# Group statistics from raw sums with their roots on GpSimd, ScalarE left to normalise, and both weight folds ahead of the spectra

## The chip, the cores and the metric

The kernel runs on one core of a Trainium2 chip. Its time is the device time of one execution in microseconds. The engines are TensorE (PE; PEld is its weight load), VectorE (DVE), ScalarE (ACT), GpSimd (POOL) and SyncE (SP), which here only issues transfers.

## What is computed

The input is (16, 16, 16, 256) float32: batch, time, width, channels. Three stages follow one another, and each adds to its input: a spectral mixing of the group-normalised input, causal attention over the 256 positions of each batch, and a mixture of eight experts of which each token takes two. The change lies wholly in the first stage and in the two weight products of the second.

```
def _gn(v, G=32, eps=1e-05):                       # groups of 8 channels, statistics over time and width
    g = v.reshape(B_, H_, W_, G, C_ // G)
    m = jnp.mean(g, axis=(1, 2, 4), keepdims=True)
    s = jnp.var(g, axis=(1, 2, 4), keepdims=True)
    return ((g - m) / jnp.sqrt(s + eps)).reshape(v.shape)
# spectral stage on xn = _gn(x)
x_ft = jnp.fft.rfft(xn, axis=-1)[..., :16]
out = x_ft * w_temb[None]                          # w_temb: time weights, sin/cos embedding @ ke_weights + ke_bias
out = jnp.einsum('btix,iox->btox', out, w)         # w: mixing weights, complex
norm = jnp.einsum('tix,iox->tox', jnp.abs(w_temb), jnp.abs(w)) + 1e-12
out = out / (jax.nn.relu(norm - 1.0) + 1.0)[None]
x = x + jnp.fft.irfft(pad(out), n=256, axis=-1)
# attention on _ln_t(x): scores from x Wq^T Wk x^T, output through Wv and Wo
# experts: softmax router, top 2 of 8, gelu, float32
```

## The kernel before

Each engine runs its own hand-written program; semaphores alone order them, and each engine executes strictly in the order written. There is no scheduler. The text below names semaphores as the code does.

**The opening (first stage).** The input lies channel-major in `xc`, 128 channels by 2 halves by 4096 tokens, and arrives in four chunks of four batches each (`ld_xc[c]`). A chunk has 8 tiles of 128x256 (`gn_tile`): four batches by two channel halves. For every chunk DVE takes the statistics of its 8 tiles (`gn_statistics`, bn_stats into `gst`), merges them into mean and variance per channel (`gn_moments`, bn_aggr into `gmv`), and turns the variance into a second moment. PE then multiplies them by a 128x128 matrix that averages 8 neighbouring channels (`group_means`, into the bank `psO`). DVE forms the group variance (`gn_variance`), ACT takes its root (L600), DVE the reciprocal and the shift (`gn_scale`), and ACT normalises the tiles in place (L604); of the last chunk DVE normalises four tiles itself (L892).

Beside that, DVE computes the angles of the time embedding (L807 to L815, then `emb_ready`), ACT its sine (L593), PE and DVE the time weights (`time_weights`), and POOL spreads the mixing weights into block matrices (L474, four each for `mix_r` and `mix_i`, L479 for `mix_abs`). The sizes of the mixing weights go DVE (L819, L821), ACT (a root, L595), DVE (`wabs_sum`, L874), POOL (L479), PE (L1259, the norm), DVE (`inv`, L884).

When the first two chunks are normalised PE takes the spectra of the first half of the positions (`spectra(0)`, L1247), and when all are, those of the second (`spectra(1)`). DVE multiplies them by the time weights (L902), PE mixes them (L1279, 32 matmuls of 256 columns), and DVE divides by the norm (L911), after which `spec` is complete and the first inverse transform can run (L1295).

**Attention.** 16 batches pass in a software pipeline of slots (`run_attention`). Ahead of it PE forms the two weight products, `fold(wq, wk)` and `fold(wv, wo_t)` (L1237, four matmuls each), one behind the mixing, one behind the first inverse transform; ACT copies them out (L612).

**Experts.** 39 groups of 256 rows, with the weights of five experts loaded while attention runs (SP, L431).

In float32 one matmul instruction shows as two records of PE and two of PEld; counts like "x8" for four matmuls are such records.

## Time and profile before

| | |
|---|---|
| median of 3 runs | 723.77 us (722.03 to 724.03) |
| the profiled execution, its own time | 726.27 us |
| its span, first to last instruction | 724.5 us |
| busy: PE, PEld | 647.4, 624.2 us |
| busy: DVE, ACT, POOL | 516.5, 413.7, 429.6 us |
| mean granted clock of TensorE | 0.964 of full speed |

The span and the execution's own time differ by 1.8 us, which lie around the first and the last instruction. The span splits into the opening (to about 57 us), attention (to about 205 us), a transition in which slots are planned (to about 242 us) and the experts. Busy shares over the whole span are averages over these four and say little about the opening, so the rows that count are those of the timeline of each engine.

### The profile page before, as it was taken

The page shows a single profiled execution, that of the slowest core. Times are in us where ns is not written, and L with a number is a line of the kernel's source. Part 1 is how long each engine was busy: PE and PEld are TensorE (multiplying, and loading weights), DVE is VectorE, ACT ScalarE, POOL GpSimd, SP SyncE. Part 2 cuts the span into 40 slices and gives each one's busy share as a digit, 9 for nine tenths or more (in the row PEclk, how much of TensorE's full clock was granted, in tenths as well). Part 3 has the DMA queues.
Part 4 walks back from the last instruction along what each step waited for, and adds up shares of the span by engine and source line. Part 5 has one row for each costly group of instructions (what it writes and reads, how often), then busy time and mean ns, then how long its engine had stood idle before and what let it go on. Part 6 is the DMA issues. An engine that isn't in the chain of part 4 may idle for free. (4 is left out here: it accounts for less than half of the span.)

```text
span 724.5 us, 16522 instructions
## 1 busy us (share of the span) xinstructions
PE 647.4 (89%) x5010; PEld 624.2 (86%) x5010; DVE 516.5 (71%) x1217; ACT 413.7 (57%) x703; POOL 429.6 (59%) x340
## 2 busy tenths in 40 slices
PE   0496999999940699999999999999999999999993
PEld 0385888888840599999999999999999999999993
DVE  8764577777764577787878777877787777777761
ACT  1804777766520556566666656565656565756550
POOL 5002326777666256766666666767676767676763
PEclk9999999999975799999999999999999999999998
DMA  8805752222323454433131313222222222232312
GB/s 343 273 0 186 276 179 74 92 90 97 106 105 113 136 162 146 96 108 59 29 59 31 57 31 57 41 47 45 43 49 39 51 37 52 36 53 35 57 19 29
DMA packets 39486, 64.13 MB, mean 89 GB/s; under 512 B 3808, under 2 KB 34848, under 8 KB 38304
## 3 DMA queue, kind: packets, MB, share of 16 engines
q0 software_dynamic: 14304, 18.92, 14.7%
q1 hardware_dynamic: 14816, 34.55, 13.5%
q10 hardware_dynamic: 10336, 10.31, 5.6%
q8 instruction: 13, 0.21, 0.1%
q14 instruction: 17, 0.14, 0.1%
HBM read 37.96 MB, written 25.81 MB: 88 GB/s over the span
## 5 line engine op out<-in xcount | busy, mean ns | idle before, releaser
L574 POOL TENSOR_TENSOR pj_lo<-w_ffn,pj_hi 128x1024 fp32r<-128x1024 f32 x78 | 189.1, 2425 | 122.8 <-ACT pj_hi L615 106.3
L1167 DVE TENSOR_TENSOR fc_lo<-w_ffn,fc_hi 128x1024 fp32r<-128x1024 f32 x78 | 116.1, 1527 | 86.2 <-ACT fc_hi L615 86.2
L564 POOL DMA_INDIRECT out<-y,add_id x78 | 121.9, 1563 | 45.1 <-issue 43.7
L615 ACT ACTIVATE pj_hi<-w_ffn 128x1024 fp32r x78 | 82.7, 1060 | 94.9 <-PE psO L1464 89.3
L615 ACT ACTIVATE fc_hi<-w_ffn 128x1024 fp32r x78 | 78.3, 1051 | 43.4 <-issue 43.4
L1464 PE MATMUL psP<-pj_hi,h_hi 128*128 128x256 f32 x312 | 91.5, 293 | 0.2 <-DVE h_lo L1167 0.2
L1464 PE MATMUL psP<-pj_hi,h_lo 128*128 128x256 f32 x312 | 88.5, 284 | 0.0
L1464 PE MATMUL psO<-pj_hi,h_lo 128*128 128x256 f32 x312 | 88.3, 283 | 0.0
L1464 PE MATMUL psO<-pj_lo,h_hi 128*128 128x256 f32 x312 | 88.3, 283 | 0.0
L1464 PE MATMUL psP<-pj_lo,h_hi 128*128 128x256 f32 x312 | 88.3, 283 | 0.0
L1464 PE MATMUL psO<-pj_hi,h_hi 128*128 128x256 f32 x312 | 88.1, 282 | 0.0
L528 POOL DMA_INDIRECT slots<-rows,slot x64 | 63.5, 993 | 19.1 <-issue 15.5
L1447 PE MATMUL psT<-x_hi,fc_hi 128*128 128x256 f32 x312 | 63.8, 287 | 5.0 <-DVE x_lo L1167 5.0
L1447 PE MATMUL psT<-x_lo,fc_hi 128*128 128x256 f32 x312 | 63.5, 286 | 0.0
L1447 PE MATMUL psT<-x_hi,fc_lo 128*128 128x256 f32 x312 | 63.5, 286 | 0.0
L1464 PEld LDWEIGHTS psP<-pj_hi,h_hi 128*128 128x128 f32 x312 | 59.8, 192 | 0.4 <-issue 0.4
L1464 PEld LDWEIGHTS psO<-pj_hi,h_hi 128*128 128x128 f32 x312 | 59.9, 192 | 0.0
L1464 PEld LDWEIGHTS psP<-pj_lo,h_hi 128*128 128x128 f32 x312 | 59.9, 192 | 0.0
L1464 PEld LDWEIGHTS psP<-pj_hi,h_lo 128*128 128x128 f32 x312 | 59.7, 191 | 0.0
L1464 PEld LDWEIGHTS psO<-pj_hi,h_lo 128*128 128x128 f32 x312 | 59.7, 191 | 0.0
L1464 PEld LDWEIGHTS psO<-pj_lo,h_hi 128*128 128x128 f32 x312 | 59.7, 191 | 0.0
L740 ACT ACTIVATE psT<-psT 128x512 f32<-128x512 f32 x78 | 45.3, 581 | 23.6 <-PE psT L1447 23.6
(252 smaller groups left out, 1639.4 us busy)
## 6 DMA issues: line engine op xcount, KB each, us to landing
w_ffn<-in_w_ffn SPq DMA_DIRECT2D x8, 2048.0 KB, 8.2
xg<-slots ACTq DMA_DIRECT2D x38, 265.0 KB
xc<-in_x_ch SPq DMA_DIRECT2D x4, 1024.0 KB, 8.9
out<-x SPq DMA_DIRECT2D x16, 256.0 KB
x<-in_x_tok SPq DMA_DIRECT2D x1, 3072.0 KB, 25.2
slots<-fill SPq DMA_DIRECT2D x9, 265.0 KB, 2.8
out<-y,add_id POOLq DMA_INDIRECT x78, 3.9
w_in<-in_w_in SPq DMA_DIRECT2D x1, 1024.0 KB, 13.7
```

The lines of the kernel that those rows point to most:

```text
L528: nc.gpsimd.indirect_dma_start(slots_d, bass.IndirectOffsetOnAxis(ap=slot[:, j, n, t % PT:t % PT + 1], axis=0), rows[:, t, :], None).then_ ...
L564: nc.gpsimd.indirect_dma_start(out_d, bass.IndirectOffsetOnAxis(ap=add_id[:, s:s + 1], axis=0), y[:, s, :], None, compute_op=ALU.add).then ...
L574: nc.gpsimd.tensor_tensor(pj_lo[:, 4 * a:4 * a + 4, :], w_ffn[:, bass.ds(e, 1), (2 + a) * DFF:(3 + a) * DFF].rearrange("p a (c d) -> p (a ...
L615: nc.scalar.activation(out, src, ACT.Copy, **kw).then_inc(done, 1)
L740: nc.scalar.activation(banks[c][:, :], banks[c][:, :], ACT.Gelu).then_inc(gelu_done, 1)
L1167: v.tensor_tensor(out, whole, upper.bitcast(F32), ALU.subtract).then_inc(done, 1)
L1447: ins = mm(banks[c][:, (f % 2) * GS:(f % 2 + 1) * GS], w[:, hh, f * P:(f + 1) * P], m[:, hh, :], start=(n == 0), stop=(n == 5))
L1464: ins = mm(bank[:, 0:D], w[:, f, s * P:(s + 1) * P], m[:, f, :], start=(f == 0 and n == 0), stop=(f == FC - 1 and n == 2))
```

## The change

The statistics are no longer merged on DVE. bn_stats leaves, for each half of a tile, a count, a mean and a sum of squared deviations. The changed kernel squares the two means into the places of the counts (`gn_squares`, one instruction), and `group_means` multiplies the raw numbers by two matrices in four matmuls that accumulate in one bank (`psS` and `psP` in turn). `gn_variance` is three instructions. The reciprocal root is one power on POOL (`inverse_root`), placed between the spreadings of the mixing weights. ACT has no root of the variance left. DVE normalises six tiles of the last chunk. Both folds stand ahead of the spectra, in banks `psO` and `psI`; the mixing into these banks waits until ACT has copied them. POOL begins to spread only after `emb_ready`. The squares of the mixing weights come behind the statistics of the second chunk, and their sum behind those of the third. SP's weight loads also wait for `idft_ready`. `conv_in` grows by the second averaging matrix, 128 columns.

```diff
-CONV_PARTS = (NG * WI * 2, NG * WI * 2, 3 * MC, DH * MC, P, 2)
+CONV_PARTS = (NG * WI * 2, NG * WI * 2, 3 * MC, DH * MC, 2 * P, 2)
+        def gn_bank(c):
+            return (psS, psP)[c % 2]
+        GN_BY_DVE = 6
...
+            pool.wait_ge(emb_ready, 1)
             pool.wait_ge(ld_conv, 16)
...
+            def inverse_root(c):
+                pool.wait_ge(gn_var, c + 1)
+                nc.gpsimd.tensor_tensor(grs[:, c, :], gvar[:, c, :], power[:, :], ALU.pow).then_inc(gn_inv, 1)
+            for g in range(NG):
+                mixing(mixr_w, mix_r, 0, g)
+            inverse_root(0)
+            for g in range(2):
+                mixing(mixi_w, mix_i, 1, g)
+            inverse_root(1)
+            for g in range(2, NG):
+                mixing(mixi_w, mix_i, 1, g)
+            inverse_root(2)
             pool.wait_ge(wabs_summed, 1)
...
+            inverse_root(3)
...
-            act.wait_ge(wabs_step, 2)
-            nc.scalar.activation(wabs[:, :], wsq[:, :], ACT.Sqrt).then_inc(wabs_ready, 1)
             act.wait_ge(temb_step, 4)
             nc.scalar.activation(tabs[:, :], tpow[:, :], ACT.Sqrt).then_inc(temb_ready, 1)
+
             for c in range(CHUNKS):
-                act.wait_ge(gn_var, c + 1)
-                nc.scalar.activation(gsd[:, c, :], gvar[:, c, :], ACT.Sqrt).then_inc(gn_sd, 1)
+                if c == 2:
+                    act.wait_ge(wabs_step, 2)
+                    nc.scalar.activation(wabs[:, :], wsq[:, :], ACT.Sqrt).then_inc(wabs_ready, 1)
                 act.wait_ge(gn_rs, c + 1)
...
+            def gn_squares(c):
+                dve.wait_ge(gn_raw, c + 1)
+                means, counts = gst[:, c, :, 1:6:3], gst[:, c, :, 0:6:3]
+                v.tensor_tensor(counts, means, means, ALU.mult).then_inc(gn_stats, 1)
             def gn_variance(c):
+
                 dve.wait_ge(gn_mm, c + 1)
...
+                v.tensor_copy(gmu[:, c, :], bank[:, CT:2 * CT]).then_inc(gn_sq, 1)
...
+                v.tensor_tensor(gsq[:, c, :], bank[:, CT:2 * CT], gmu[:, c, :], ALU.mult).then_inc(gn_sq, 1)
...
+                v.scalar_tensor_tensor(gvar[:, c, :], bank[:, 0:CT], GN_EPS, gsq[:, c, :], ALU.add,
+                                       ALU.subtract).then_inc(gn_var, 1)
+            def gn_shift(c):
+                dve.wait_ge(gn_inv, c + 1)
+                v.scalar_tensor_tensor(gnb[:, c, :], gmu[:, c, :], -1.0, grs[:, c, :], ALU.mult, ALU.mult).then_inc(gn_rs, 1)
+            gn_statistics(0, range(CT))
+            gn_squares(0)
             time_weights()
+            gn_variance(0)
             for c in range(1, CHUNKS):
+                gn_statistics(c, range(4))
+                if c > 1:
+                    gn_variance(c - 1)
+                else:
+                    gn_shift(0)
+                gn_statistics(c, range(4, CT))
+                gn_squares(c)
+                if c > 1:
+                    gn_shift(c - 1)
+                if c == 1:
+                    wabs_squares()
+                if c == 2:
+                    wabs_total()
             gn_variance(CHUNKS - 1)
+            gn_shift(CHUNKS - 1)
...
+            group_means(0)
+            group_means(1)
+            pe.wait_ge(ld_qkvo, 16)
+            fold(wq, wk, psO)
+            group_means(2)
+            fold(wv, wo_t, psI)
 
             pe.wait_ge(temb_step, 2)
             pe.wait_ge(gn_done, 2 * CT)
-            spectra(0)
-            pe.wait_ge(gn_done, 3 * CT + CT // 2)
-            pe.wait_ge(gn_done_dve, CT // 2)
+            spectra(0, range(0, 2))
+            group_means(CHUNKS - 1)
+            spectra(0, range(2, NG))
+            norms()
+            pe.wait_ge(gn_done, 4 * CT - GN_BY_DVE)
+            pe.wait_ge(gn_done_dve, GN_BY_DVE)
             spectra(1)
```

What stands in a row on each engine is shown at three places. DVE before, from the moments of the second chunk to the statistics of the last (`gst` are the raw statistics, `ggm` the group means, `gnb` the shift whose end releases ACT):

```order
L868 SCALAR_TENSOR_TENSOR gnb<-ggm,grs 128x8
L845 BN_STATS gst<-xc 128x6 x8
L859 COPY ggm<-psO 128x16
L860 TENSOR_TENSOR gsq<-ggm 128x8
L861 TENSOR_TENSOR gvar<-ggm,gsq 128x8
L862 TENSOR_SCALAR gvar<-gvar 128x8
L851 BN_AGGR gmv<-gst 128x2 x8
L854 TENSOR_TENSOR gsq<-gmv 128x8
L855 TENSOR_TENSOR gmv<-gmv,gsq 128x8
L867 RECIPROCAL grs<-gsd 128x8
L868 SCALAR_TENSOR_TENSOR gnb<-ggm,grs 128x8
L845 BN_STATS gst<-xc 128x6 x8
```

DVE now, over the same stretch, from the variance of the second chunk (bank `psP`) to that of the third (`psS`):

```order
L883 COPY gmu<-psP 128x8
L885 TENSOR_TENSOR gsq<-psP,gmu 128x8
L887 SCALAR_TENSOR_TENSOR gvar<-psP,gsq 128x8
L869 BN_STATS gst<-xc 128x6 x4
L877 TENSOR_TENSOR gst<-gst 128x16
L893 SCALAR_TENSOR_TENSOR gnb<-gmu,grs 128x8
L851 TENSOR_REDUCE wabs_sum<-wabs 128x16
L869 BN_STATS gst<-xc 128x6 x4
L883 COPY gmu<-psS 128x8
L885 TENSOR_TENSOR gsq<-psS,gmu 128x8
```

The sum `wabs_sum`, which stood ahead of the second chunk's statistics, now stands between the second chunk's shift and the last chunk's statistics. ACT before, from the sine to the third chunk:

```order
L593 ACTIVATE emb<-ang 32x16
L595 ACT_TABLE_LOAD
L595 ACTIVATE wabs<-wsq 128x64
L597 ACTIVATE tabs<-tpow 128x16
L600 ACTIVATE gsd<-gvar 128x8
L604 ACTIVATE xc<-xc,gnb,grs 128x256 x8
L600 ACTIVATE gsd<-gvar 128x8
L604 ACTIVATE xc<-xc,gnb,grs 128x256 x8
```

and ACT now:

```order
L616 ACTIVATE emb<-ang 32x16
L618 ACT_TABLE_LOAD
L618 ACTIVATE tabs<-tpow 128x16
L627 ACTIVATE xc<-xc,gnb,grs 128x256 x16
L623 ACTIVATE wabs<-wsq 128x64
L627 ACTIVATE xc<-xc,gnb,grs 128x256 x10
```

The root `wabs`, which `wabs_sum` reads, moved from ahead of all tiles to behind the sixteenth. PE now, from the first averages to the second half of the spectra (before, the three `group_means` had no fold between them, and the folds stood behind the mixing):

```order
L1266 MATMUL psP<-gst,conv_in 128x16 x2
L1268 MATMUL psP<-gst,conv_in 128x8
L1269 MATMUL psP<-gst,conv_in 128x8
L1274 MATMUL psO<-w_in 128x256 x4
L1266 MATMUL psS<-gst,conv_in 128x16 x2
L1268 MATMUL psS<-gst,conv_in 128x8
L1269 MATMUL psS<-gst,conv_in 128x8
L1274 MATMUL psI<-w_in 128x256 x4
L1284 MATMUL psT<-xc,conv_in 32x128 x16
```

Each chunk's averages are four matmuls where there was one, and the two folds stand around those of the third chunk.

## Rows read from the trace of the kernel before

**Rows 1.** The page: busy time by engine, and PE over 40 slices of the span.

```profile
PE 647.4 (89%) x5010; PEld 624.2 (86%) x5010; DVE 516.5 (71%) x1217; ACT 413.7 (57%) x703; POOL 429.6 (59%) x340
...
PE   0496999999940699999999999999999999999993
```

**Rows 2.** Windows: length, busy PE, PEld, DVE, ACT, POOL, then granted clock, DMA share, GB/s.

```profile
8.00:9.00 1.00, 0.00 (x0) 0.00 (x0) 1.00 (x4) 0.11 (x1) 1.00 (x2) 1.00 1.04 422
...
35.00:38.00 3.00, 3.00 (x54) 2.55 (x58) 1.51 (x4) 1.44 (x2) 0.00 (x0) 0.50 0.03 8
...
62.00:65.00 3.00, 2.74 (x10) 2.09 (x9) 1.77 (x6) 0.60 (x1) 1.10 (x2) 0.50 0.99 426
100.00:115.00 15.00, 15.00 (x98) 13.47 (x97) 11.81 (x53) 10.66 (x26) 5.88 (x8) 1.00 0.25 87
```

**Rows 3.** Timeline of DVE, opening: start, length, what, idle before it.

```profile
4.33 0.95 DVE L814 TENSOR_SCALAR ang<-ang,time_in 32x16 f32<-32x16 f32 x1
5.32 0.98 DVE L815 SCALAR_TENSOR_TENSOR ang<-ang,time_in 32x16 f32<-32x16 f32 x1
...
7.47 2.71 DVE L845 BATCH_NORM_STATS2 gst<-xc 128x6 f32<-128x256 f32 x8
...
16.71 0.17 DVE L859 COPY ggm<-psO 128x16 f32<-128x16 f32 x1
...
18.58 0.17 DVE L868 SCALAR_TENSOR_TENSOR gnb<-ggm,grs 128x8 f32<-128x8 f32 x1
...
32.39 0.20 DVE L867 RECIPROCAL grs<-gsd 128x8 f32<-128x8 f32 x1 [2.36 <-ACT gsd L600]
...
32.85 1.38 DVE L892 TENSOR_SCALAR xc<-xc,ggm,grs 128x256 f32<-128x256 f32 x4
```

**Rows 4.** Timeline of ACT, opening.

```profile
7.85 0.26 ACT L595 ACTIVATE wabs<-wsq 128x64 f32<-128x64 f32 x1
...
18.78 4.04 ACT L604 ACTIVATE xc<-xc,gnb,grs 128x256 f32<-128x256 f32 x8 [1.05 <-DVE gnb L868]
...
32.84 2.07 ACT L604 ACTIVATE xc<-xc,gnb,grs 128x256 f32<-128x256 f32 x4 [0.49 <-DVE gnb L868]
```

**Rows 5.** Timeline of POOL: spreading, opening.

```profile
4.21 4.22 POOL L474 TENSOR_TENSOR mix_r<-conv_in 128x512 f32<-128x512 f32 x4 [3.33 <-DMA conv_in<-in_conv_in]
```

**Rows 6.** POOL's groups, shapes apart: the power of two columns, a copy.

```profile
L505 POOL TENSOR_TENSOR rs<-rs,power 128x2 f32<-128x2 f32 x32 | 22.7, 711 | 40.9 <-DVE rs L946 38.6 <-issue 2.3
L559 POOL COPY add_id<-slot_id 128x2 int32 x37 | 7.0, 189 | 0.0
```

**Rows 7.** Timeline of PE: opening and start of attention; last, one row of its middle.

```profile
23.64 1.87 PE L1259 MATMUL psI<-tabs,mix_abs 128*128 128x16 f32 x8
...
31.25 1.15 PE L1247 MATMUL psV<-xc,conv_in 128*32 128x128 f32 x16
34.97 2.11 PE L1247 MATMUL psT<-xc,conv_in 128*32 128x128 f32 x32 [2.58 <-ACT xc L604]
...
37.74 1.18 PE L1247 MATMUL psV<-xc,conv_in 128*32 128x128 f32 x16
38.85 0.70 PE L1279 MATMUL psS<-zr,mix_r 128*128 128x256 f32 x2
...
52.77 1.89 PE L1237 MATMUL psS<-w_in 128*128 128x256 f32 x8
...
61.65 0.78 PE L1307 MATMUL psT<-ident,xn 128*128 128x128 f32 x4 [2.83 <-ACT xn L674]
...
63.12 3.10 PE L1317 MATMUL psG<-xn_t,qk_w 128*128 128x256 f32 x8 [0.26 <-ACT xn_t L615]
...
103.43 0.96 PE L1336 MATMUL psT<-attn_in,xn_t 128*128 128x8 f32 x8
```

**Rows 8.** Transfers by line: KB each, us from issue to landing.

```profile
w_in<-in_w_in SPq DMA_DIRECT2D x1, 1024.0 KB, 13.7
```

**Rows 9.** Issue of the first chunk and its landing, window 1.6 to 2.1.

```profile
xc<-in_x_ch SPq DMA_DIRECT2D x1, 1024.0 KB, 5.8
...
1.69 0.43 SPq L411 DMA_DIRECT2D xc<-in_x_ch  x1
```

More of the change, by code:

```diff
@@ L108, in constants @@
     return {
-        "dft": dft.astype(f), "masks": masks.astype(f), "group": np.kron(np.eye(P // 8), np.full((8, 8), 1 / 8)).astype(f),
+        "dft": dft.astype(f), "masks": masks.astype(f), "group": np.concatenate([np.kron(np.eye(P // 8), np.full((8, 8), 1 / n)) for n in (16, 8 * SEQ)], axis=1).astype(f),
         "angles": angles.astype(f), "causal": causal.astype(f), "counting": counting.astype(f), "experts": experts.astype(f),
@@ L177, in hybrid_block @@
         dft = dft.rearrange("p (h m) -> p h m", h=DH)
+        group = group.rearrange("p (n q) -> p n q", n=2)
         idft = cv("idft", [MC, D])
@@ L209, in hybrid_block @@
         x = at("x", [P, NT, D])
[L210 removed]
+        power = at("power", [P, 8])
         attn_in = at("attn_in", [P, sum(ATTN_PARTS)])
@@ L848, in gn_moments @@
-            def gn_moments(c):
-                for n in range(CT):
-                    ins = v.bn_aggr(gmv[:, c, n, :], gst[:, c, n, :])
-                gn_link(ins)
-                mean, var = gmv[:, c, :, 0], gmv[:, c, :, 1]
-                gn_link(v.tensor_tensor(gsq[:, c, :], mean, mean, ALU.mult))
-                v.tensor_tensor(var, var, gsq[:, c, :], ALU.add).then_inc(gn_stats, 1)
+                if n == CT - 1:
+                    ins.then_inc(gn_raw, 1)
+            def gn_squares(c):
+                dve.wait_ge(gn_raw, c + 1)
+                means, counts = gst[:, c, :, 1:6:3], gst[:, c, :, 0:6:3]
+                v.tensor_tensor(counts, means, means, ALU.mult).then_inc(gn_stats, 1)
@@ L870, in _ @@
-            gn_statistics(0)
-            gn_moments(0)
-            dve.wait_ge(wabs_ready, 1)
-            v.tensor_reduce(wabs_sum[:, :], wabs[:, :].rearrange("p (g o) -> p o g", g=NG), AX_X, ALU.add).then_inc(wabs_summed, 1)
+                bank = gn_bank(c)
+                v.tensor_copy(gmu[:, c, :], bank[:, CT:2 * CT]).then_inc(gn_sq, 1)
+                dve.wait_ge(gn_sq, 2 * c + 1)
+                v.tensor_tensor(gsq[:, c, :], bank[:, CT:2 * CT], gmu[:, c, :], ALU.mult).then_inc(gn_sq, 1)
@@ new lines, in _ @@
+                if c == 1:
+                    wabs_squares()
+                if c == 2:
+                    wabs_total()
+            gn_variance(CHUNKS - 1)
+            gn_shift(CHUNKS - 1)
+            dve.wait_ge(gn_rs, CHUNKS)
+            for n in range(CT - GN_BY_DVE, CT):
+                tile = gn_tile(CHUNKS - 1, n)
+                v.tensor_scalar(tile, tile, grs[:, CHUNKS - 1, n:n + 1], gnb[:, CHUNKS - 1, n:n + 1], ALU.mult,
+                                ALU.add).then_inc(gn_done_dve, 1)
@@ L883, in _ @@
             dve.wait_ge(norm_mm, 1)
[L884 removed]
+            v.tensor_scalar(inv[:, :], psS[:, 2 * CT:2 * CT + NG * HT], 1e-12, 1.0, ALU.add, ALU.max).then_inc(inv_step, 1)
             dve.wait_ge(inv_step, 1)
             v.reciprocal(inv[:, :], inv[:, :]).then_inc(inv_ready, 1)
[L887 to L893 removed]
@@ L1228, in group_means @@
                 pe.wait_ge(gn_stats, c + 1)
-                if c:
-                    pe.wait_ge(gn_var, c)
-                mm(psO[:, 0:2 * CT], group[:, :], gmv[:, c, :, :], start=True, stop=True).then_inc(gn_mm, 1)
+                if c > 1:
+                    pe.wait_ge(gn_var, c - 1)
+                bank = gn_bank(c)
+                for n in range(2):
+                    mm(bank[:, 0:2 * CT], group[:, 0, :], gst[:, c, :, 3 * n:3 * n + 2].rearrange("p n k -> p k n"),
+                       start=(n == 0), stop=False)
+                mm(bank[:, 0:CT], group[:, 1, :], gst[:, c, :, 2], start=False, stop=False)
+                mm(bank[:, 0:CT], group[:, 1, :], gst[:, c, :, 5], start=False, stop=True).then_inc(gn_mm, 1)
             def fold(w, m, bank):
@@ L1239, in fold, with spectra @@
                 ins.then_inc(qkvo_mm, 1)
-            def spectra(half):
+            def spectra(half, groups=range(NG)):
                 cols = slice(half * SEQ // 2, (half + 1) * SEQ // 2)
-                for g in range(NG):
+                for g in groups:
                     for j in range(4):
```

102 lines of the change are left out of this document (37 added, 65 removed).

## The prediction

> **What bounds the kernel now.** I read the page first. PE is the busiest engine, and its slices are full from the fourth on, but for a dip in the middle [rows 1]; in the middle of attention a window of 15 us shows it busy all 15 us at the full granted clock [rows 2]. So attention and the experts run at PE's pace and are not touched by the change. What the opening gains or loses is passed on whole, as long as nothing at the start of attention swallows it. The chain of waits in the page covers only the last microseconds, so for the opening I read the timelines of the engines. There PE waits 2.58 us for the last normalised tiles and starts the second half of the spectra at 34.97 [rows 7]. **That start, 34.97, is the mark against which I reckon the change**, and the first mixing matmul at 38.85 the next one. Behind it nothing changes until attention but the places of the folds.
>
> What leads to 34.97: ACT needs 4.04 us for eight tiles, 0.505 each, and idles between chunks [rows 4]. DVE is the slower one. Its first statistics start at 7.47 and take 2.71; from the variance of the first chunk at 16.71 to the end of its shift at 18.75 it spends 2.04 us on small instructions, most of 0.17 [rows 3]. Per chunk that makes 4.7. At the end it waits 2.36 for ACT's root, then ACT takes four tiles in 2.07 and DVE four in 1.38 [rows 3, 4].
>
> **What the change removes.** Between two chunks' statistics DVE keeps one square (0.17), three for the variance (0.51) and one shift (0.17), with 0.04 between dependent ones about 1.05 us instead of 2.04. ACT's roots and the wait of 2.36 go. The embedding chain is also freed: L814 and L815 take 0.95 and 0.98 where their like take 0.17, and they end at 5.28 and 6.30, one spreading of 1.05 apart, that began on POOL at 4.21 [rows 3, 5]. A DVE instruction that reads SBUF beside POOL's product waits until that product is done; statistics do not (2.71 under the same cover). With POOL held back to `emb_ready`, this is ready near 4.75. But the first chunk lands at 1.69 + 5.8 = 7.49 [rows 9], 0.16 later with 64 KB more in front at 422 GB/s [rows 2], so the statistics start at 7.65 and nothing of this comes through.
>
> **What it adds, step by step, at a power of 0.72 us.** Chunk 0: statistics to 10.36, square to 10.57. The averages are four matmuls; the norm has just as many, and took 1.87 [rows 7]; done 12.5. Variance to 13.1, power to 13.9. The shift wants to run at 14.4, but POOL has started a spreading at 13.9 and holds it until 15.0. ACT starts its tiles there instead of at 18.78. Chunk 1: the rest of its statistics and square to 16.6, the two squares of the mixing weights, averages at 18.5, variance 19.1, power 19.9, statistics of chunk 2 to 20.4, square held to 21.0, shift held by the second spreading to **22.05**. ACT has been idle since 19.1.
>
> Now the order decides. ACT normalises chunk 1 until 26.1, then takes the root `wabs`, 0.26 [rows 4], and DVE, which stands at `wabs_sum` with the last statistics queued behind, **waits from 22.05 to 26.3**. Before, that sum stood ahead of all this and waited for nothing. Then: sum 26.6, half the statistics 27.9, variance 28.5, power 29.25, the other half 29.75; `mix_abs` on POOL (1.05) holds the square to 30.4, shift 30.6. ACT: chunk 2 and two tiles, 10 x 0.505, to **35.7**. DVE: averages (0.95 to 1.87), variance, power, shift 32.9 to 33.8, six tiles of 0.345, to **35.1 to 35.9**. PE: averages, 32 spectra records (2.0), norm (0.95 to 1.87): 34.3 to 36.2. So the spectra's second half starts at 35.7 to 36.2 instead of 34.97: **+0.7 to +1.2**. The earlier start of 3.7 us is spent in the wait of 4.3 and the three held shifts.
>
> **The power.** The trace has it only for two columns, 0.711 [rows 6]; here it has eight. Bound below: all of it is start-up, 0.71. Above: it grows in proportion beyond a copy of two columns (0.189), 0.189 + 4 x 0.522 = 2.3. POOL multiplies 512 columns in 1.05 [rows 5], so columns are cheap to it, and I take 1.0, nearer the lower. It counts about three times (chunks 0 and 1 through the held shifts, chunk 3 alone): the start goes to 36.5 to 37.2 at 1.0, and to 39.4 to 40.3 at 2.3. Taken: 36.6, **+1.6**.
>
> **The clock.** At 23.6 the profile's clock reads full, but eight records of weight-bound matmuls take 1.87 there and 0.96 in attention [rows 7]: the early stretch is at the lower level, 1.2 GHz. In 35 to 38 it is granted 0.50 [rows 2], after 2.58 idle. In the changed kernel the folds keep PE busy from 18.5 to 27 and the averages, spectra and norm from 30.4 on, so the second half will mostly run at 2.4 GHz. What is it worth? The last 16 records (from 37.74, 1.18) straddle the rise, the same ones of the first half (from 31.25, 1.15) were wholly at the lower level: no gain [rows 7]. I take 0 to -0.4, say **-0.2**. The Trainium skill ("TensorE: Matmul & The Clock Gate", The HAM clock gate) measures back-to-back matmuls twice as fast at the higher level; by that the half would take 1.94 instead of 3.88. The same section gives about 62 ns per matmul as the sequencer's floor where hardware decoding is off, which by 64 records in 3.88, 61 ns each, would leave it at 3.88.
>
> **The folds** (four matmuls, 1.89 each at full clock, about 3.5 at half) move into idle time of PE: the weights land at 4.0 + 13.7 = 17.7 [rows 8], and the last spectra wait for ACT at 26.1 anyway. Where they left they were covered as well: the first by DVE's division after 52.77, the second by the normalisation, behind which PE idled 2.83 before 61.65 [rows 7]. Worth 0. But they kept PE active: now it idles from the end of the mixing to 61.65 but for one inverse transform. It ran 62 to 65 at 0.50 already [rows 2], L1317 taking 3.10 against 1.89 of an equal fold; I add **+0.3**, between 0 and 1.7. ACT copies the folds at 36 to 37.5, before the mixing reaches psO. SP's loads start some 2 us earlier, behind nothing that PE waits for. POOL's inverse parts run at about 34 to 36, far before 55.
>
> **Sum.** +1.6 - 0.2 + 0.3 = +1.7 us. The profiled execution took 726.27, 2.5 over the median of 723.77; its own would become 728.0. On the median: 725.4.
>
> **The rivals.**
> - *The wait on the root costs what I say, and the power is cheap or middling* (0.7 to 1.3): +0.5 to +2.5, 724.3 to 726.3. Chance 0.47.
> - *The power grows with columns* (1.5 to 2.3): +2.5 to +5.3, up to 729. For it: 0.711 for two columns against 0.189 for a copy. Against it: 512 products in 1.05. Chance 0.23.
> - *Faster: the spectra are clock-bound after all.* PE has the folds in front, so the second half runs at 2.4 GHz and takes 1.94: -1.9 against +1.6 + 0.3, 723.8; with the power at 0.72 (+0.7) it is 722.8. It decides from the point where the start lies below 36.6. Past -2.2 it gets only if POOL's products do not hold the shifts either: without the holds the start is 33.6, -1.3, together -3.0, 720.8. For it: weight-bound rows halve. Against it: the group across the rise did not. Chance 0.18, of which 0.12 beyond the bound below.
> - *The start of attention stays one stretch longer at the lower clock*: +1.7 more, 727. Chance 0.12.
>
> A change under 0.3%, 2.2 us, can hardly be told from none. The first case lies mostly inside it; faster 0.13, same 0.47, slower 0.40. The range reaches from the fast rival's 721.5 to the slow power's 729.
>
> **What will show it.** Right: DVE idle 4 us ahead of `wabs_sum`, released by ACT; ACT idle some 4 us after its sixteenth tile; shifts of near 1 us ending with a POOL product; L1284's second half starting near 36.5. The power's mean at 128x8 settles the second case; the length of the second half (3.9 or 2) the third; L1365's first four matmuls (3.1 or more) the fourth. Wrong would be a sum that does not wait, or first mixing matmuls before 38.

## The result, and the profile after

The changed kernel is slower, by a little: ratio 1.0048 (95% 1.0036 to 1.0060) to the kernel before in the same session, or 3.5 us. Its median over nine runs is 726.62 us, against 722.05 for nine runs of the kernel before; two of its nine were disturbed by the machine (1670 and 756 us) and don't enter the ratio, and the median of the other seven is 725.89. Two later sessions gave 1.0031 and 1.0041. The profiled execution took 726.62, its span is 724.5; the forecast was 725.4.

The page's totals and the windows that answer to [rows 1, 2]; the last column but two is the granted clock:

```profile
PE 655.2 (90%) x5034; PEld 631.3 (87%) x5034; DVE 514.4 (71%) x1175; ACT 411.8 (57%) x697; POOL 435.7 (60%) x344
...
37.00:40.00 3.00, 2.86 (x52) 2.61 (x56) 2.35 (x8) 2.31 (x4) 0.00 (x0) 0.50 0.00 0
64.00:67.00 3.00, 2.74 (x9) 2.27 (x10) 1.27 (x3) 0.60 (x1) 1.10 (x2) 0.50 0.51 115
100.00:115.00 15.00, 15.00 (x95) 13.34 (x93) 12.03 (x61) 9.94 (x22) 4.47 (x7) 1.00 0.08 27
```

DVE and ACT each lost 2 us of work and POOL gained 6; attention's middle is unchanged. The totals say nothing of why it is slower. DVE's timeline of the opening does (answers to [rows 3]):

```profile
4.65 0.22 DVE L838 SCALAR_TENSOR_TENSOR ang<-ang,time_in 32x16 f32<-32x16 f32 x1
7.54 2.71 DVE L869 BATCH_NORM_STATS2 gst<-xc 128x6 f32<-128x256 f32 x8 [2.67 <-DMA xc<-in_x_ch]
12.49 0.17 DVE L883 COPY gmu<-psS 128x8 f32<-128x8 f32 x1 [1.32 <-PE psS L1269]
14.85 1.02 DVE L893 SCALAR_TENSOR_TENSOR gnb<-gmu,grs 128x8 f32<-128x8 f32 x1 [0.48 <-POOL grs L489]
...
21.29 0.18 DVE L877 TENSOR_TENSOR gst<-gst 128x16 f32<-128x16 f32 x1
21.70 1.00 DVE L893 SCALAR_TENSOR_TENSOR gnb<-gmu,grs 128x8 f32<-128x8 f32 x1 [0.22 <-POOL grs L489]
26.95 0.26 DVE L851 TENSOR_REDUCE wabs_sum<-wabs 128x16 f32<-128x64 f32 x1 [4.25 <-ACT wabs L623]
...
30.75 1.00 DVE L893 SCALAR_TENSOR_TENSOR gnb<-gmu,grs 128x8 f32<-128x8 f32 x1 [0.22 <-POOL grs L489]
...
34.37 2.63 DVE L919 TENSOR_SCALAR xc<-xc,grs,gnb 128x256 f32<-128x256 f32 x6
```

The embedding chain is freed, 0.22 each for L837 and L838 against 0.95 and 0.98 [rows 3], and nothing comes of it, since the first chunk still lands at 7.5. The row with 4.25 in its bracket is the wait at `wabs_sum`, released by ACT. The three shifts (L893) of 1.00 to 1.02 are the held ones. The fourth, of the last chunk, takes 0.33, from 34.01 on; no product runs then, but a cast of POOL's that ends at 34.31. A shift beside which POOL does nothing takes 0.17 (below). On ACT the other half of the same knot (answers to [rows 4]), and POOL with the powers and products that hold the shifts (answers to [rows 5, 6]):

```profile
15.91 4.04 ACT L627 ACTIVATE xc<-xc,gnb,grs 128x256 f32<-128x256 f32 x8 [4.48 <-DVE gnb L893]
22.74 4.04 ACT L627 ACTIVATE xc<-xc,gnb,grs 128x256 f32<-128x256 f32 x8 [2.79 <-DVE gnb L893]
26.68 0.24 ACT L623 ACTIVATE wabs<-wsq 128x64 f32<-128x64 f32 x1
31.79 5.04 ACT L627 ACTIVATE xc<-xc,gnb,grs 128x256 f32<-128x256 f32 x10 [4.87 <-DVE gnb L893]
```

```profile
13.14 1.68 POOL L489 TENSOR_TENSOR grs<-gvar,power 128x8 f32<-128x8 f32 x1 [4.10 <-DVE gvar L887]
14.80 2.06 POOL L481 TENSOR_TENSOR mix_i<-conv_in 128x512 f32<-128x512 f32 x2
20.02 1.64 POOL L489 TENSOR_TENSOR grs<-gvar,power 128x8 f32<-128x8 f32 x1 [3.17 <-DVE gvar L887]
21.63 2.07 POOL L481 TENSOR_TENSOR mix_i<-conv_in 128x512 f32<-128x512 f32 x2
```

PE (answers to [rows 7]) starts the spectra's second half, the mark of the prediction, at 37.14 instead of 34.97:

```profile
19.19 3.76 PE L1274 MATMUL psO<-w_in 128*128 128x256 f32 x8
...
23.86 1.97 PE L1274 MATMUL psI<-w_in 128*128 128x256 f32 x8
26.92 2.08 PE L1284 MATMUL psT<-xc,conv_in 128*32 128x128 f32 x32 [1.09 <-ACT xc L627]
...
33.56 1.07 PE L1296 MATMUL psS<-tabs,mix_abs 128*128 128x16 f32 x8
37.14 2.08 PE L1284 MATMUL psT<-xc,conv_in 128*32 128x128 f32 x32 [2.52 <-DVE xc L919]
...
41.03 0.70 PE L1327 MATMUL psS<-zr,mix_r 128*128 128x256 f32 x2
```

DVE's six tiles of the last chunk end last, at 37.00 (ACT's at 36.83), and the first two of them are held too, until POOL's cast and product for the inverse transform are done. These two tiles take 0.54 and 0.88, the other four 0.40 each:

```profile
34.37 0.54 DVE L919 TENSOR_SCALAR xc<-xc,grs,gnb 128x256 f32<-128x256 f32 x1
34.83 0.88 DVE L919 TENSOR_SCALAR xc<-xc,grs,gnb 128x256 f32<-128x256 f32 x1
34.84 0.72 POOL L515 TENSOR_TENSOR idft_parts<-idft,idft_parts 32x256 fp32r<-32x256 f32 x1
```

Where the loss goes from there is read from six marks of each profile. They are, in us: first statistics; the spectra's second half; attention's first value product (L1327 before, L1375 after); attention's last matmul row; the copy of `counts`; and, further on, the end of the last expert matmul.

| | stats | 2nd half | value | last | counts | end |
|---|---|---|---|---|---|---|
| before | 7.47 | 34.97 | 66.06 | 204.54 | 221.94 | 712.19 |
| before_again | 7.43 | 35.11 | 66.48 | 204.95 | 222.36 | 708.92 |
| before_third | 7.44 | 35.04 | 66.82 | 205.31 | 222.71 | 716.56 |
| after | 7.54 | 37.14 | 68.57 | 207.04 | 224.43 | 712.26 |
| again | 7.13 | 36.73 | 68.55 | 207.04 | 224.45 | 712.61 |
| after_third | 7.14 | 36.75 | 68.61 | 208.36 | 225.45 | 715.70 |

Against the first profile of before the end is where it was, though 2.5 us are lost by `counts`. That profile was a long one: its own time lies 2.5 us over the median, and the second one shows why (below). Against the second (own time 722.97), the change costs 2.03 at the mark, 2.09 at both ends of attention, 2.07 at `counts`, 3.34 at the end. In the third profile of the changed kernel 1.3 us more are lost between the value product and attention's last row: 139.75 there, where the five others take 138.47 to 138.49. From 206 us on it was granted 0.50, before_third 1.00.

### The profile page after: what moved, and what is told of

The parts are those of the page before. It is cut to its first block and busy times, and to the rows that moved or that the text cites. A ratio compares the mean times of both kernels' runs of the same rounds, so it can differ in the third digit from the quotient of the medians.

```text
span 724.5 us, 16522 instructions
## 1 busy us (share of the span) xinstructions
PE 655.2 (90%) x5034; PEld 631.3 (87%) x5034; DVE 514.4 (71%) x1175; ACT 411.8 (57%) x697; POOL 435.7 (60%) x344
## 5 line engine op out<-in xcount | busy, mean ns | idle before, releaser
L1199 DVE TENSOR_TENSOR fc_lo<-w_ffn,fc_hi 128x1024 fp32r<-128x1024 f32 x78 | 118.0, 1551 | 89.6 <-ACT fc_hi L638 89.5
L1505 PE MATMUL psP<-pj_hi,h_hi 128*128 128x256 f32 x312 | 92.2, 295 | 0.0
L1505 PE MATMUL psP<-pj_hi,h_lo 128*128 128x256 f32 x312 | 89.1, 286 | 0.0
L1505 PE MATMUL psO<-pj_lo,h_hi 128*128 128x256 f32 x312 | 88.9, 285 | 0.0
L1505 PE MATMUL psO<-pj_hi,h_lo 128*128 128x256 f32 x312 | 88.8, 285 | 0.0
L1505 PE MATMUL psP<-pj_lo,h_hi 128*128 128x256 f32 x312 | 88.8, 285 | 0.0
L1505 PE MATMUL psO<-pj_hi,h_hi 128*128 128x256 f32 x312 | 88.6, 284 | 0.0
L1505 PEld LDWEIGHTS psP<-pj_lo,h_hi 128*128 128x128 f32 x312 | 60.6, 194 | 0.0
L1505 PEld LDWEIGHTS psO<-pj_hi,h_hi 128*128 128x128 f32 x312 | 60.6, 194 | 0.0
L1505 PEld LDWEIGHTS psP<-pj_hi,h_hi 128*128 128x128 f32 x312 | 60.5, 194 | 0.0
L1505 PEld LDWEIGHTS psO<-pj_hi,h_lo 128*128 128x128 f32 x312 | 60.4, 194 | 0.0
L1505 PEld LDWEIGHTS psP<-pj_hi,h_lo 128*128 128x128 f32 x312 | 60.3, 193 | 0.0
L1505 PEld LDWEIGHTS psO<-pj_lo,h_hi 128*128 128x128 f32 x312 | 60.3, 193 | 0.0
```

The source lines that it names most:

```text
L1199: v.tensor_tensor(out, whole, upper.bitcast(F32), ALU.subtract).then_inc(done, 1)
L1505: ins = mm(bank[:, 0:D], w[:, f, s * P:(s + 1) * P], m[:, f, :], start=(f == 0 and n == 0), stop=(f == FC - 1 and n == 2))
```

## The experiments

**The changed kernel again**, with no edit.

> The changed kernel once more, to read its opening in a second execution. Both traces so far agree on the opening: the second half of the spectra starts at 37.14 instead of 34.97 (+2.17), and by the second batch's query weights attention is 2.5 us late. The medians differ by about 3.5. If the opening is the whole cause, the start lies at 37.1 again and the difference of the times is 2.5 +- 0.5; the 1 us more was then chance in where the plan behind attention waits. Rival: something behind the opening costs another 1 us each time; then the difference is again 3.5 and a later stretch (attention, the plan or the first expert group) is regularly longer.

726.77 against 723.92, ratio 1.0031 (1.0018 to 1.0044). Its opening is in the table: 29.60 us from first statistics to the mark, as in the first profile (29.60); before 27.50 and 27.68. The third profiles have 29.61 and 27.60. So the opening's loss of 2.0 us is a property of the kernel and not of one execution.

**The root of the mixing weights one chunk earlier**, to remove the wait at `wabs_sum`:

```diff
-                if c == 2:
+                if c == 1:
                     act.wait_ge(wabs_step, 2)
```

> The root of the mixing weights' sizes one chunk earlier on ACT, ahead of its ninth tile instead of its seventeenth. Theory (the misplaced root makes DVE wait 4.25 us at its sum, and the last statistics behind it): the wait goes, the start of the second half falls from 37.1 to about 35.1, the time by 2.0. It does not fall by the whole 4.25, since the averages of the last chunk then stand behind the first spectra on PE and the last power behind mix_abs on GpSimd. Rival (the folds or the clock cost it, the wait lies in slack): start unchanged at 37.1, time unchanged.

The wait is gone, but the mark came only to 36.12, 1.0 before the changed kernel's 37.14 and 0.75 before it counted from first statistics; ratio to before 1.0018 (1.0006 to 1.0031). What took its place is on PE:

```profile
24.05 3.58 PE L1274 MATMUL psI<-w_in 128*128 128x256 f32 x8
27.56 2.07 PE L1284 MATMUL psT<-xc,conv_in 128*32 128x128 f32 x32
29.56 0.62 PE L1266 MATMUL psP<-gst,conv_in 128*128 128x16 f32 x4
```

The last averages (L1266) stand behind the second fold and half of the first spectra in PE's program, and reach PE at 29.56. DVE had its chunk's statistics long before and waits 3.1 us for them (L883 at 30.66). A part is the clock: the second fold takes 3.58 here and 1.97 in the changed kernel's first profile. One wait of 4.25 hid another of 3.1: the idle time in front of an instruction is not what its removal gives.

**All spreadings ahead of the first inverse root** on POOL:

```diff
-            inverse_root(0)
-            for g in range(2):
+            for g in range(NG):
                 mixing(mixi_w, mix_i, 1, g)
+            inverse_root(0)
             inverse_root(1)
-            for g in range(2, NG):
-                mixing(mixi_w, mix_i, 1, g)
             inverse_root(2)
```

> All eight spreadings of the mixing weights ahead of the first power, where GpSimd idles 4 us anyway, and none between the powers. Theory (a GpSimd product holds the DVE instruction that reads SBUF): the shifts of chunks 0 and 1 take 0.2 instead of 1.0, ACT starts its second chunk 1.6 to 1.7 us earlier and the start of the second half falls from 37.1 to 35.5, the time by 1.6. The wait of 4.25 at the sum stays, as it depends on ACT's eight tiles alone. Rival (the long shifts are long for another reason, their operands): they stay at 1.0, nothing moves by more than 0.3.

Mark 35.24, 28.15 from first statistics: 1.45 less than 29.60, as expected. The time doesn't show it: 725.59, ratio 1.0030 (1.0015 to 1.0045), against 1.0031 for the unchanged kernel beside it, with intervals of 1 us either way. Of the 1.45 us this profile gave none back by `counts` (215.38 from first statistics, 216.89 and 217.32 in the changed kernel). The first two shifts (L891 in this kernel) are free, the third is still held by `mix_abs`, and the squares of the time weights pay instead, under cover of PE's averages:

```profile
10.34 0.66 DVE L858 TENSOR_TENSOR tsq<-temb 128x32 f32<-128x32 f32 x1
11.03 0.96 DVE L860 TENSOR_TENSOR tpow<-tsq 128x16 f32<-128x16 f32 x1
12.05 0.17 DVE L881 COPY gmu<-psS 128x8 f32<-128x8 f32 x1
...
14.65 0.17 DVE L891 SCALAR_TENSOR_TENSOR gnb<-gmu,grs 128x8 f32<-128x8 f32 x1 [0.72 <-POOL grs L489]
...
28.85 1.00 DVE L891 SCALAR_TENSOR_TENSOR gnb<-gmu,grs 128x8 f32<-128x8 f32 x1 [0.22 <-POOL grs L489]
```

That the hold is POOL's product, and not the shift's own work, is thereby shown: one shift, moved away from the product, goes from 1.02 to 0.17.

**The folds back in their old places** (and their old banks), the rest of the change kept:

```diff
-            fold(wq, wk, psO)
             group_means(2)
-            fold(wv, wo_t, psI)
...
+                if k == -1:
+                    fold(wv, wo_t, psP)
+                    pe.wait_ge(qkvo_ready, 2)
...
+            fold(wq, wk, psS)
```

> Only the two folds back where they stood, behind the mixing and behind the first inverse transform. Theory (the folds are covered in both places and cost only the clock at the start of attention): start of the second half unchanged at 37.1; from the last mixing matmul to the second value product some 0.3 us less, the time 0 to 0.5 lower. Rival (the front folds hold up PE in the opening): the start falls by 1 us or more, with the averages of the third chunk ready earlier and used.

726.37, ratio 1.0034 (1.0020 to 1.0049), against 1.0031 for the unchanged one beside it. The mark did not stay where I expected it: 37.54, 30.42 from first statistics, 0.8 later than with the folds in front. Without them PE comes to the last averages at the lower pace. The four matmuls take 1.87 instead of 1.06, and DVE waits for them:

```profile
30.17 1.03 PE L1266 MATMUL psP<-gst,conv_in 128*128 128x16 f32 x4 [1.58 <-DVE gst L877]
32.08 0.17 DVE L883 COPY gmu<-psP 128x8 f32<-128x8 f32 x1 [0.75 <-PE psP L1269]
```

Mark to value product 31.38 against 31.43, 31.82 and 31.86. The folds take 1.89 each in both gaps, where PE would have idled. So in front they gain 0.8 us of the opening in this profile, by the clock alone, and the time of the whole kernel does not tell the two places apart.

**Root early and spreadings first together.**

> The two moves together: the root of the sizes one chunk earlier, and all eight spreadings ahead of the first power. Alone, the first brought the start of the second half from 37.1 to 36.1 (not 35.1: the last averages came to stand behind the second fold, at the lower clock, and the first spectra on PE), the second to 35.2. Theory (both cost, and with both gone PE's order binds): start between 33.2 and 34.7, the time 2.5 to 4 below the changed kernel, level with before or up to 1.5 us under it. Rival (the second is hidden behind PE's order once the first is gone): 35.2 to 36, time 1.5 below the changed kernel.

729.75 against 728.11, ratio 1.0028 (1.0011 to 1.0046). Mark 35.20, 28.40 from first statistics: no better than the spreadings alone, so the rival of the expectation came. The same order on PE binds. The last averages end at 29.7, and DVE waits for them:

```profile
29.74 0.17 DVE L881 COPY gmu<-psP 128x8 f32<-128x8 f32 x1 [2.95 <-PE psP L1267]
```

**All moves**: the two above, the last averages ahead of all spectra, `mix_abs` ahead of its second inverse root, five tiles on DVE instead of six.

```diff
-        GN_BY_DVE = 6
+        GN_BY_DVE = 5
...
-            inverse_root(2)
             pool.wait_ge(wabs_summed, 1)
...
                 ALU.mult).then_inc(mix_built, 1)
+            inverse_root(2)
...
+            group_means(CHUNKS - 1)
...
-            spectra(0, range(0, 2))
-            group_means(CHUNKS - 1)
-            spectra(0, range(2, NG))
+            spectra(0)
```

> The two moves, mix_abs ahead of the third power, the last averages ahead of the first spectra on PE, and five tiles of the last chunk on DVE instead of six. Theory (what is left of the delay is order: the last averages behind spectra, a shift held by mix_abs): the shift of the third chunk takes 0.2, the last averages start at 25 to 27, the second half at 31.3 to 32.6, some 3 us earlier than before (34.97); the time 0.3 to 0.5% under before. Rival (the first half of the spectra and the norm then fill PE, and the averages moved forward only push them): start at 33.5 or later, less than 0.2% under before.

Mark 31.57, 3.4 before the kernel before's, but value product only 2.4 and `counts` 1.9 earlier; 727.84 against 728.11, ratio 0.9985 (0.9965 to 1.0005), which decides nothing and is less than the 0.3 to 0.5% that I expected. PE idles only 0.33 ahead of the second half here, keeps its clock, and takes no less for it, 3.90 to the first mixing matmul at 35.47:

```profile
31.60:35.50 3.90, 3.90 (x65) 2.57 (x65) 3.07 (x9) 2.12 (x4) 0.33 (x1) 1.00 0.41 138
```

Run once more:

> The changed kernel with the four moves (root of the mixing weights after chunk 1, all spreadings ahead of the inverse root, `mix_abs` ahead of its second inverse root and the last averages ahead of the spectra, five instead of six tiles on DVE), a second time, because its first comparison, 0.9985 with 0.9965 to 1.0005, could not tell it from the kernel before. My theory, that the opening is passed on but for about 1.5 us given back at the start of attention: counts 1.9 us before those of the kernel before, and a ratio of 0.9974, 0.9985 at most. The rival, that a lower clock in attention or the experts eats the whole opening: ratio 1.000 or above, with the counts at 222 or the experts 1.6 us longer. The plan behind attention takes 6.6 or 14 us here whatever the kernel if (b) of the run beside it holds.

722.27 against 723.91, ratio 0.9982 (0.9970 to 0.9995): a real gain over the kernel before, of 1.3 us. The profile agrees with before_again: value product 65.13 against 66.48, `counts` 221.01 against 222.36, both 1.35 earlier. That is less than the 1.9 and the ratio of 0.9974 of my expectation. The same program placed its mark at 33.23 here and at 31.57 in the first profile. The rows that differ are the second fold, in the first profile and in the repeat:

```profile
22.98 1.97 PE L1272 MATMUL psI<-w_in 128*128 128x256 f32 x8
```

```profile
23.28 3.76 PE L1272 MATMUL psI<-w_in 128*128 128x256 f32 x8
```

The fold delays the averages behind it by its own lower clock. Counted from first statistics the first profile is 1.5 us ahead of the repeat at the mark (24.67 and 26.16), 1.3 at the value product (56.73 and 58.06, 59.05 in before_again) and 0.8 at attention's end (195.77 and 196.53). Only 0.2 of the 0.7 us given up lie at the start of attention; the other 0.6 lie in its last batches (139.04 us from value product to last row, 138.48 in the repeat), whose cause these profiles leave open. So my theory, that 1.5 us are given back at the start of attention, did not hold: against before_again the repeat gives back 0.5 there (1.88 ahead at the mark, 1.35 at the value product). The gain at the mark is real but depends on the second fold's clock.

**All moves, folds back in their old places.**

> As the kernel before this one in the list, with the two folds back behind the mixing and behind the first inverse transform. Theory (the front folds now stand between the averages, and their 3.5 us at the lower clock cost there; behind the mixing they are covered): start of the second half at 31.3 to 32, the same or up to 1 us earlier than with the folds in front, attention's start 0.2 to 0.5 faster; time 0.4 to 0.6% under before. Rival (the folds in front raise the clock for the first spectra and the norm, and that is worth something): start 0.5 to 1 us later than with them.

727.93 against 728.11, ratio 0.9981 (0.9958 to 1.0004), where I expected 0.4 to 0.6% less; mark 31.67, value product 64.02. From first statistics the mark is at 24.65, like the profile with the fast fold in front (24.67) and 1.5 before the one with the slow fold (26.16). In time it is within its interval the same as with the folds moved.

**The power on two columns of eight.** `grs` is set to 1.0 and only two columns are raised, so six of eight tiles are normalised without their root:

```diff
-                nc.gpsimd.tensor_tensor(grs[:, c, :], gvar[:, c, :], power[:, :], ALU.pow).then_inc(gn_inv, 1)
+                nc.gpsimd.tensor_tensor(grs[:, c, 0:2], gvar[:, c, 0:2], power[:, 0:2], ALU.pow).then_inc(gn_inv, 1)
```

> The changed kernel with the power on two of each chunk's eight columns; the other six keep the inverse root 1, so six tiles in eight are not divided by their deviation. Its time is the changed kernel's but for the width of the power. Theory (0.155 us a column, and every power stands in a path): the power takes 0.71 instead of 1.64 to 1.68, the shift of chunk 0 ends 0.9 earlier, that of the last chunk 0.9 earlier again, the start of the second half falls by 1.5 to 1.8, the time by 1.6. Rival (only the last power is in a path, the first ones lie behind statistics): start 0.9 earlier.

The power takes 0.69 to 0.73 instead of 1.64 to 1.68:

```profile
12.54 0.73 POOL L490 TENSOR_TENSOR grs<-gvar,power 128x2 f32<-128x2 f32 x1 [3.56 <-DVE gvar L888]
...
18.48 0.70 POOL L490 TENSOR_TENSOR grs<-gvar,power 128x2 f32<-128x2 f32 x1 [3.16 <-DVE gvar L888]
```

The mark is 27.17 from first statistics instead of 29.60: 2.4 earlier for 0.95 less per power, so the mark moves by some two and a half times the power, more than I had expected of this run. A part of that is the holds. With the short power the square meets the product and takes 0.48 instead of 0.18, and the shift then comes to stand between two products and takes 0.15 instead of 1.00:

```profile
19.75 0.48 DVE L878 TENSOR_TENSOR gst<-gst 128x16 f32<-128x16 f32 x1
20.15 0.15 DVE L894 SCALAR_TENSOR_TENSOR gnb<-gmu,grs 128x8 f32<-128x8 f32 x1
```

At 0.7 us per power the changed kernel's mark lies before that of the kernel before (27.50 to 27.68). The time decides nothing: 730.87 of eight runs, ratio 1.0029 (1.0004 to 1.0053), an interval that holds both the changed kernel's 1.0041 and the 1.6 us less that I expected. The session was one where the plan behind attention was drawn out (next). Value product 59.07 from first statistics, in the changed kernel 61.03 to 61.47. Behind it this profile loses 1.4 us between value product and last row (139.86), granted 0.50 from 203.6 to 206.8, as the third profile of the changed kernel does, and 1.2 in the first expert projection (24 matmuls at the lower clock, see below).

**The kernel before, a second and third profile**, and **the changed one a third time**, with no edit. They answer two questions: why the first two profiles end together, and where 1.3 us beyond `counts` come from.

> The kernel before, unchanged, profiled a second time. Two readings of its first profile are open. In it the second half of the spectra starts at 34.97, the counts are copied at 221.94 and `late_need` at 236.25, 14.3 us later, where the changed kernel took 6.6 us for the same instructions. (a) If the 14.3 us belong to the kernel before (to its program, or to where its instructions lie), it shows them again, and the changed kernel has gained time there that hides part of its loss. (b) If they belong to the execution or the chip, this profile may show 6.6 as well, and then its own time should come out near its median instead of 2.5 us above. I expect (b), at 2 in 3, and in both cases 35.0 +- 0.4 for the spectra, 222 +- 0.4 for the counts, and a ratio of 1.000 within 0.0015 in time.

> The kernel before, unchanged, a third profile. Its second one was 3.3 us shorter than its first, because the plan took 6.6 us instead of 14.3, and in both TensorE reached its full clock after some 12 of the 0.41 us matmuls of the experts' first second projection; both profiles of the changed kernel reached it only after some 24, which costs about 1.3 us. Theory: that is the execution's phase and no property of the kernel, so over more profiles either kernel shows both, and the change's own cost is the 2.1 us of the opening. Rival: it belongs to the kernels, early again here and late again in the run beside it; then it is a real part of the measured 3.5 us. I give the rival 0.5, since two profiles against two is what there is. Counts 87.0 us before the end of a plan that took 6.6, or 14 if the plan is drawn out again; ratio 1.000 within 0.0015.

> The changed kernel, unchanged, a third profile beside a third one of the kernel before. Opening as in the first two: second half of the spectra 29.6 us after the first statistics, attention's last matmul at 207.0 against 204.5 to 204.95. Theory: the late rise of the clock in the experts' first second projection (24 matmuls of 0.41 us instead of 12, 1.3 us) is the execution's phase, and may be missing here. Rival: it is the kernel's, and stands here again. Time: 1.003 to 1.005 of the kernel before in either case, since the ratio is measured over many executions: nearer 1.003 by the theory, 1.005 by the rival.

before_again: 723.29 against 723.91 (0.9994); its plan from `counts` to `late_need` takes 6.61 us, against 14.31 in the first profile and 15.93 in the third. before_third: 729.49 against 730.32 (0.9996). after_third: 8.27. The same rows of DVE, first profile and second:

```profile
225.75 0.48 DVE L1138 TENSOR_REDUCE plan<-past 128x39 f32<-128x312 f32 x1 [0.90 <-DVE past_end L1137]
...
233.48 0.20 DVE L1149 SCALAR_TENSOR_TENSOR plan<-plan 128x39 f32<-128x39 f32 x1 [1.22 <-DVE plan L1148]
```

```profile
224.74 0.48 DVE L1138 TENSOR_REDUCE plan<-past 128x39 f32<-128x312 f32 x1
...
227.46 0.20 DVE L1149 SCALAR_TENSOR_TENSOR plan<-plan 128x39 f32<-128x39 f32 x1
```

The instructions take the same time; idle time lies between them. Reading (b) of the expectation holds: the long plan does not belong to the kernel. It goes mostly with the session: the six profiles of the two sessions with medians near 724 have 6.6 us, the four of the session at 728 have 14.1 to 15.0. The session at 730 has 15.9 and 8.3, the first one 14.3 and 6.6. It explains why the two kernels' first profiles end together, though of its 7.7 us more only 3.3 reach the end, since the first expert group then runs some 4 us faster.

The second question is the experts' first second projection (L1464 before, L1505 after). PE begins it at 1.2 GHz; its first matmul, one at the lower and one at the full clock, in the changed kernel:

```profile
250.15 0.56 PE L1505 MATMUL psP<-pj_hi,h_hi 128*128 128x256 f32 x1
...
255.20 0.41 PE L1505 MATMUL psO<-pj_hi,h_lo 128*128 128x256 f32 x1
255.41 0.31 PE L1505 MATMUL psP<-pj_hi,h_hi 128*128 128x256 f32 x1
255.56 0.28 PE L1505 MATMUL psP<-pj_lo,h_hi 128*128 128x256 f32 x1
```

There the lower clock lasts 24 matmuls, and the projection takes 8.16 us to the next matmul (250.15 to 258.31); in before_again 11, and 6.95 (248.03 to 254.98). That is the 1.2 us that the pair differs by beyond `counts`. In after_third it rose after 9, in before_third after 10 (after 3 in the first profile of before), and the session's ratio is 1.0041 (1.0022 to 1.0059). So the late rise is not in every execution of the changed kernel, and the kernel with all moves, one program, shows both: 22 in its first profile, 10 in the repeat. Whether it is more frequent in the changed kernel (two of three profiles, against none of three) these few profiles leave open. One expectation of after_third failed: attention's last row is at 208.36 and not at 207.0, by the 1.3 us at the lower clock named under the table.

## Why the prediction was right within its range, and which case came

The time, 1.2 us off (0.5 against the 725.89), lies well inside the range. That closeness is in part luck. I added +1.7 to 723.77, the median of three runs; nine runs in the session of the result gave 722.05. Against its own kernel before the change costs 3.5 us where I had said 1.7. And the case that came is the second, of which I said 0.23: its power of 1.5 to 2.3 us holds the measured 1.64 to 1.68, near its lower end, and its +2.5 to +5.3 us holds the 3.5 and 3.0 of two comparisons and nearly the 2.2 of the third. It holds the whole kernel only, with what comes behind attention; the opening alone costs 2.0 to 2.1, less than the 2.5 with which this case begins. The first case, my likeliest, had the same mechanism with a power of 0.7 to 1.3.

**The mechanism and the place.** DVE idle 4.25 ahead of `wabs_sum`, released by ACT; ACT idle 4.87 after its sixteenth tile; shifts of 1.00 to 1.02. Start of the statistics forecast 7.65, found 7.54. Averages 12.5 and 12.49. First shift free at 15.0, found 15.87. Second 22.05 and 22.70. Sum 26.3 and 26.95. Mark 36.6, in a range of 36.5 to 37.2 at the power I took, and 37.14 found. Term by term:

- *The power* was mis-sized: 1.0 taken, 1.64 to 1.68 measured. It grows with the columns (0.70 for two, 1.66 for eight; a line through these two is 0.16 a column and 0.38 to start), so the choice "nearer the lower" end, by the products' cheap columns, was the step that failed. A factor of three on the difference, 0.66, would have given a mark of 38.6, which did not come.
- *What made up for it:* the holds. At 0.72 I had, for the second and third chunk, the square held by one product and, in the second, the shift by the next. At 1.66 the square ends beside the power, unheld (L877 at 21.29 takes 0.18 while the power runs from 20.02 to 21.66), and only the shift is held, once. So 0.94 us more per power moved the first shift's end by 0.9, the second's by 0.65, the third's by 1.15 and the last tiles' by 1.1, and did not count three times. At the short power itself the forecast was too late: power_2_columns has the mark 27.17 after the first statistics, where the steps at 0.72 give 28.05 to 28.55, since the shift slipped in between two products. Two errors, the power too short and the holds too long, offset each other. That too is luck.
- *The last stretch:* I had the last averages and the norm at 0.95 to 1.87; they took 1.06 and 1.07 (L1296), at the full pace. DVE's six tiles took 2.63, 0.44 each and not 0.345, since two were held by POOL's inverse parts; I had looked only at when these are needed, not at what they hold.
- *The clock* (-0.2): nothing. The second half took 3.89 from 37.14 to 41.03, before 3.88; granted 0.50, after PE had idled 2.52 in front of it. With all moves, granted 1.00 and right behind a norm at the full pace (1.06), it took 3.90. The same matmuls in the first half, from 26.92, between a fold at the full pace (1.97) and a norm at the full pace (1.07), took 2.08 for 32 as well, as in the second half before, 2.11 [rows 7]. So the third rival, the faster kernel, was wrong in its premise: these matmuls gain nothing from 2.4 GHz. With the sequencer's floor that the prediction quoted from the Trainium skill ("TensorE: Matmul & The Clock Gate", The HAM clock gate), about 62 ns each, the trace agrees nearly (57 to 61 ns); the doubling does not show on these shapes.
- *The folds* (0 in place, +0.3 at the start of attention): mark to value product 31.43, 31.82 and 31.86 against 31.09, 31.37 and 31.78 before. The means differ by 0.3, as forecast, but profiles of one kernel differ by more. Their place was not worth exactly 0 in the opening: in front they raise the clock of the last averages (0.8 us by folds_back). Both folds_back and all_moves_folds_back give the same time as with the folds moved.
- *From the profile to the median:* the step that subtracted 2.5 because the profiled execution lay above the median held, and before_again showed the cause.

**Sum against result.** Forecast +1.7. The opening costs 2.1 at `counts`, of which power, folds and clock account as above. The whole kernel showed 3.5, 2.2 and 3.0 us in three comparisons (each ratio by its time). The rest, 0.1 to 1.4, lies behind the opening. In the profiles the lower clock costs something at two places there: 1.2 us in the first expert group (first and second profile of the changed kernel) and 1.3 at the end of attention (the third). That the change causes either is not shown. I had no term for what comes behind the opening but the +0.3. What came is just beyond the 2.2 us of no change, so the sign was the one I gave 0.40 and not the 0.47.

**The rivals.** Ahead of attention the clock did stay at the lower level for longer, some 10 us (57.5 to 67.7) instead of 3.4 (62.0 to 65.4). From 58 to 62 us the kernel before is granted 1.00 and the changed one 0.50:

```profile
58.00:62.00 4.00, 1.17 (x7) 0.76 (x6) 1.33 (x6) 2.10 (x4) 1.27 (x2) 1.00 0.56 143
58.00:62.00 4.00, 0.77 (x2) 0.50 (x2) 2.47 (x8) 0.41 (x1) 1.18 (x3) 0.50 0.86 270
```

But PE has next to nothing to do there, and the fourth case's 1.7 us did not come: the first eight records of the query weights (L1365, L1317 before) took 2.93, 3.28 and 3.78 in three profiles, and 3.10, 3.50 and 3.68 before.

## What to carry to other kernels

When work moves from one in-order engine to another, write down for each engine what now stands in front of what: here ACT had no more roots of groups, but one root of weights stayed behind eight tiles, and DVE's sum with two chunks of statistics queued behind it. Moving that one root is a line, and shows the next order that binds (PE's averages behind a fold); only all the moves together turned 0.3 to 0.5% slower into 0.2% faster, and which of them could be left out was not tried. Write down too what a side job holds while it runs: a product or a cast of POOL's that nobody waits for yet lengthened DVE's shifts and tiles. Moving a matmul into idle time of an engine is worth nothing in itself if it left idle time as well, but it changes the clock at which its neighbours run.

Take two profiles of each kernel before believing a difference of some us in a stretch that the change doesn't touch: here the same kernel's plan took 6.6, 14 or 16 us.

## What the runs showed of the hardware

- GpSimd's power costs by the column: 0.69 to 0.73 us for 128x2, 1.64 to 1.68 for 128x8, where a product of 512 columns takes 1.05.
- A small DVE instruction with both inputs in SBUF waits for a GpSimd product to end (1.02 against 0.17), but runs freely beside a GpSimd power. A DVE normalisation of a tile, with one tile as input, is held as well (0.88 beside a product, 0.54 beside a cast, 0.40 otherwise); statistics are not. The Trainium skill ("GPSIMD Engine Reference", Specifications) names contention between the two for DVE instructions with two SBUF inputs; the products agree, the power (L877: 0.18 beside it) doesn't.
- Float32 matmuls that load 32 columns and stream 128 follow one another every 57 to 61 ns at 1.2 as at 2.4 GHz (64 in 3.89 and 3.90 us); with 128 columns loaded, eight took 3.76 at the lower and 1.97 at the full pace.
- In the first 32 us the profile's granted clock reads 1.00 whether the fold takes 3.76 or 1.97 and the four averages 1.87 or 1.06: the column can't be used there, and the duration of a known shape must be.
- A chain of some 25 small DVE instructions took 6.6, 8.3 or 14 to 16 us in different executions, the long ones with idle time of 0.2 to 1.2 us between dependent ones. The cause stays open; it wasn't the kernel.
- The lower clock at the end of attention (0.50 from 206 us) cost one execution of the changed kernel 1.3 us that two others of the same program did not pay.
